# First loads of x and gate weights as one transfer each, with later loads held behind them, in a gated FFN on one core

## The reference

```
w = weights[conditions]                       # one 32x32 matrix per batch
y = einsum('bct,bcd->bdt', x, w)
h = silu(y @ w_gate) * (y @ w_up)             # 256 -> 1024
h_sparse = of each 4 neighbours, keep the 2 largest by magnitude
out = x + h_sparse @ w_down                   # 1024 -> 256
```

## Time and profile before

| | us |
|---|---|
| median of 3 runs | 83.6 (83.55 to 83.94) |
| the profiled execution's own time | 83.66 |
| its span (first to last instruction of the program) | 81.7 |
| PE busy | 75.5 (92%) |
| DVE busy | 61.2 (75%) |
| ACT busy | 42.9 (53%) |
| granted TensorE clock, mean | 0.994 of full |

### The profile page before, as it was taken

How to read it: one execution, slowest core, us unless ns; L and a number is a source line. 1 busy time by engine, 2 the same in 40 slices (tenths; PEclk the granted TensorE clock), 3 DMA queues, 4 the chain that set the end, 5 groups by cost and what they waited for, 6 DMA issues and landing times.

```text
span 81.7 us, 983 instructions
## 1 busy us (share of the span) xinstructions
PE 75.5 (92%) x338; PEld 59.8 (73%) x338; DVE 61.2 (75%) x93; ACT 42.9 (53%) x65; POOL 8.0 (10%) x13
## 2 busy tenths in 40 slices
PE   3996699999999999999999999999999999999920
PEld 1331688898888888888888888888888888888800
DVE  0003799178389999996899999999999999991060
ACT  6000983595863986975392699995770006410000
POOL 7500000000000070013000000442000000000000
PEclk9999999999999999999999999999999999999997
DMA  0792899977400049915800000399950000006024
GB/s 0 138 326 113 251 325 335 429 237 285 201 0 0 0 88 199 195 32 96 160 4 0 8 4 0 64 193 201 205 108 0 0 0 0 0 0 257 0 92 164
DMA packets 3076, 9.62 MB, mean 118 GB/s; under 512 B 480, under 2 KB 480, under 8 KB 2816
## 3 DMA queue, kind: packets, MB, share of 16 engines
q1 hardware_dynamic: 2160, 6.29, 22.3%
q0 software_dynamic: 912, 3.28, 20.9%
HBM read 5.37 MB, written 1.05 MB: 79 GB/s over the span
## 4 chain that ended last, share of the span: by engine, by line
PE 84%; DMA 8%; DVE 3%; ACT 1%; issue 1%; DVEq 0%
PE bank L536 50%; PE y_banks L573 13%; PE bank L573 13%; DMA h<-in_table,rows_sb 5%; PE y_banks L521 5%; PE bank L547 4%; DMA cond_sb<-in_cond 2%; DVE gate_raw L428 2%; ACT h L237 1%; DVE h L347 1%; DVE rows_sb L432 0%; DVEq L427 0%
## 5 line engine op out<-in xcount | busy, mean ns | idle before, releaser
L536 PE MATMUL bank<-y_hl,up_hl 128*128 128x512 f32 x96 | 24.2, 389 | 0.0
L536 PE MATMUL bank<-y_hl,gate_hl 128*128 128x512 f32 x84 | 21.4, 390 | 0.0
L536 PEld LDWEIGHTS bank<-y_hl,up_hl 128*128 128x128 f32 x96 | 18.0, 188 | 3.8
L536 PEld LDWEIGHTS bank<-y_hl,gate_hl 128*128 128x128 f32 x84 | 15.7, 188 | 3.2
L243 ACT ACTIVATE silu<-bank 128x512 f32<-128x512 f32 x16 | 9.4, 595 | 8.5 <-PE bank L536 8.2
L264 ACT ACTIVATE h_hl<-h 128x1024 fp32r<-128x1024 f32 (+1 forms) x8 | 6.7, 844 | 8.5 <-DVE h L414 8.4
L573 PE MATMUL y_banks<-h_hl,down_hl 128*128 128x512 f32 x48 | 11.0, 389 | 0.0
L573 PE MATMUL bank<-h_hl,down_hl 128*128 128x512 f32 x48 | 11.0, 389 | 0.0
L573 PEld LDWEIGHTS y_banks<-h_hl,down_hl 128*128 128x128 f32 x48 | 9.0, 188 | 1.9
L573 PEld LDWEIGHTS bank<-h_hl,down_hl 128*128 128x128 f32 x48 | 9.0, 188 | 1.9
L378 DVE TENSOR_TENSOR h<-bank,silu 128x512 f32<-128x512 f32 x12 | 8.1, 684 | 1.9 <-ACT silu L243 1.9
(11 more groups left out here) (40 smaller groups left out, 71.9 us busy)
## 6 DMA issues: line engine op xcount, KB each, us to landing
h_hl<-h POOLq DMA_DIRECT2D x4, 512.0 KB, 5.2
up_raw<-in_w_up SPq DMA_DIRECT2D x2, 512.0 KB, 5.8
down_raw<-in_w_down SPq DMA_DIRECT2D x1, 1024.0 KB, 9.5
gate_raw<-in_x_t SPq DMA_DIRECT2D x1, 1024.0 KB, 5.0
down_hl<-down_raw POOLq DMA_DIRECT2D x2, 512.0 KB, 5.5
out<-gate_raw SPq DMA_DIRECT2D x4, 256.0 KB, 2.3
x_sb<-in_x SPq DMA_DIRECT2D x2, 256.0 KB, 4.0
gate_raw<-in_w_gate SPq DMA_DIRECT2D x2, 256.0 KB, 4.4
```

What stands on the lines that cost most here:

```text
L536: last = nc.tensor.matmul(dst, w_hl[w][:, s, q, k, j], y_hl[:, m, half, k], start=i == 0, stop=i == len(terms) - 1)
```

## The change

The first half of x is loaded by one transfer of 128 x 4 KB pieces in place of two of 128 x 2 KB, and so are the gate weights of q = 0, with one semaphore for all of it. SP waits for those gate weights as well as for `mix_in` before it issues the up weights of q = 0, and then waits until these have landed before it issues the second half of x and what follows. ACT splits the gate weights ahead of its three blocks of the diagonal, and `WARM_START` goes from 18 to 16.

```diff
-    WARM_START = 18
+    WARM_START = 16
...
-        w_in = [[None, sem("gate_in1")], [sem(f"up_in{q}") for q in range(NQ)]]
-        first_in = [sem(f"first_in{k}") for k in range(KT)]
+        w_in = [[sem(f"gate_in{q}") for q in range(NQ)], [sem(f"up_in{q}") for q in range(NQ)]]
...
-            for g in range(0, GH, 2):
-                sp.dma_start(x_sb[:, g:g + 2, :], x[:, g:g + 2, :]).then_inc(x_in[0], 16)
-            for k in range(KT):
-                sp.dma_start(raw_w[0][:, 0, k], w_gate[:, 0, k]).then_inc(first_in[k], 16)
-
+            sp.dma_start(x_sb[:, 0:GH, :], x[:, 0:GH, :]).then_inc(x_in[0], 16)
+            sp.dma_start(raw_w[0][:, 0], w_gate[:, 0]).then_inc(w_in[0][0], 16)
+
+            sp.wait_ge(w_in[0][0], 16)
             sp.wait_ge(mix_in, 16)
             sp.dma_start(raw_w[1][:, 0], w_up[:, 0]).then_inc(w_in[1][0], 16)
+            sp.wait_ge(w_in[1][0], 16)
             sp.dma_start(x_sb[:, GH:NG, :], x[:, GH:NG, :]).then_inc(x_in[1], 16)
...
             def high_weights(q, w, k, end):
-                act.wait_ge(first_in[k] if (q, w) == (0, 0) else w_in[w][q], 16)
+                act.wait_ge(w_in[w][q], 16)
...
-            diagonal(ACT_FIRST)
             for piece in PIECES[:KT]:
                 high_weights(*piece)
+            diagonal(ACT_FIRST)
             for piece in Y_PIECES[:KT]:
                 high_y(*piece)
...
             def low_weights(i):
                 q, w, k, end = PIECES[i]
-                dve.wait_ge(first_in[k] if (q, w) == (0, 0) else w_in[w][q], 16)
+                dve.wait_ge(w_in[w][q], 16)
...
             def mixing(half):
-                pe.wait_ge(x_in[half], 32 if half == 0 else 16)
+                pe.wait_ge(x_in[half], 16)
```

## The result

The changed kernel takes 83.38 us (median of 14 runs, 83.02 to 83.72), the kernel before, run beside it, 83.86 (14 runs, 83.50 to 84.56). The ratio is 0.9948, with a 95% interval of 0.9925 to 0.9971: 0.44 us faster, between 0.24 and 0.63.

The account below looks back on a forecast made before the run. PE was taken to bound the kernel, its start held by the gather behind 1 MB of loads. Terms -0.55 +0 +0.2 +0 = -0.35 gave 83.3 from 83.66 and 83.25 from the median; forecast 83.2 us, range 82.6 to 84.0.

Parts of the forecast that it names:

- The reading that the gather stands in line: Start of the kernel: the gather is last behind 1 MB of x and gate weights and lands 0.35 us after them.
- The rival that the queues take turns: At the gather: it lands well ahead of the gate weights, PE starts at 8.1, time 82.9 us; chance 0.06.
- the rule that the prediction quotes for it: Trainium skill on DMA queues: each DMA engine takes turns between queues that have work, packet by packet.
- Part 1: First loads as one transfer each of 4 KB pieces: gather lands at 6.90, PE starts at 8.31, 0.55 us earlier.
- one slow stretch: First transfers from 2.2 to 4.3 us, moving 151 GB/s in the kernel before, against 295 in the later burst.
- the reading behind the 0.25: First loads: the slowness belongs to POOL's issue of the gather, so only the rest gets quicker, 0.25 us earlier.
- The reading behind the 0.85: First loads: they move like the later 1 MB burst in 4 KB pieces, landing at 6.25 for 7.1, 0.85 us earlier.
- Part 2: Gate splits ahead of the diagonal on ACT, before mixing(0): cost nothing, with 0.2 us of cover.
- Part 3: SP's wait for up weights before x's second half: up weights of q = 1 land at 17.5, PE waits 0.2 us at pair 3.
- The estimate from the Trainium skill: SP's later loads: 2.0 us plus bytes at 436 GB/s gives 3.2 us for up weights, 5.6 for the next 1.5 MB, no wait.
- Part 4: Two fewer matmuls on zeros at the start: PE idles 1.28 us before mixing(0); nothing gained, nothing lost.
- The rival of the clock: PE before mixing(0): without an earlier gather, 1.83 us idle could drop the clock to 1.2 GHz, 85.5 us; chance 0.02.

Follow-up runs that it names:

- The late gather: Kernel before with POOL zeroing the diagonal three times, so the gather is issued at 4.35 instead of 2.98; one execution, 83.77 us.
- diagonal first: Changed kernel with ACT's three blocks of the diagonal ahead of its gate splits, as before; 83.37 us, ratio 0.9942.
- the hold alone: Kernel before with only SP's added wait for the up weights ahead of the second half of x; 84.08 us, ratio 1.0032.
- four issues: Kernel before with x and gate weights of q = 0 in 4 KB pieces, two transfers of 64 partitions each; 84.92 us, ratio 1.0130.
- x alone: Changed kernel with only x's first half ahead of the gather, no held transfers, diagonal first, 14 matmuls on zeros; 84.66 us, ratio 1.0108.

## Why the prediction was right

**What bounds the start.** The reading that the gather stands in line behind what SP issued held with 0.75 MB and more ahead: 0.75 MB, 6.15; 1 MB, 6.85 to 6.95 in 4 KB pieces (7.30 in one execution) and 7.45 in 2 KB ones; 1.5 MB, 8.5; each about 0.35 behind the last of them. It does not reach further: with 0.5 MB ahead the gather lands at 6.17, 0.91 behind x, and issued 1.4 us later it takes 3.1 us. There the gather's own time is the limit, 3.1 to 3.2 us from its issue, which the prediction left out. It did no harm, as the gather issued at 2.98 was to land at 6.90. The rival that the queues take turns, and with it the rule that the prediction quotes for it, falls with 1.5 MB ahead: the gather had its 3.2 us behind it at 6.2, and still landed behind all of it.

**Part 1, 0.55 earlier.** Measured 0.50. The value was the middle of 0.25 and 0.85, two readings of one slow stretch. The late gather shows that the reading behind the 0.25 was false: the slowness does not belong to POOL's issue (that it has to do with POOL's other work isn't excluded, as POOL zeroed in that stretch). The reading behind the 0.85, the rate of the later burst (295 GB/s), was too high: the first burst reached 209. So the number came out right by luck, as a middle of two readings neither of which holds; the mechanism (4 KB pieces in one transfer move the first megabyte sooner, and the gather with it) did hold. What sets 209 against 295 is open. That the one-transfer loads do it is shown by the run with them alone. Whether it is the size of the pieces as such is not settled, as each other way of moving these bytes brought a cost of its own; fewer issues alone are not it.

**Part 2, ACT's order, nothing.** Right: diagonal first gives 83.37. The blocks came 0.18 behind DVE's copies, and the first was ready ahead of the third copy, as worked out. All three were done by 8.49, ahead of PE's third group near 8.86. (The prediction's 0.5 us to that group is two of eight groups' products, four rows of 16, not four of eight; the time is right.)

**Part 3, the hold, 0.2.** Measured 0.16 in the block of pairs, 0.26 and 0.30 in two other kernels with the hold, and 0.27 (0.02 to 0.51) in the time when the hold stands alone. The up weights took 3.5 us for 3.2 predicted, and those of q = 1 landed 6.75 behind the burst's first issue for 7.35: at 17.3 for 17.5 predicted. product(0) ended at 20.33 for 20.5. The estimate from the Trainium skill, DMA: Bandwidth & Descriptors, section Anatomy of one DMA (3.2 us and 5.6 us), was near for the first and 1.15 too short for the second, and would have left no wait where there was one.

**Part 4, two matmuls less.** No effect was seen; the runs with 18 and with 16 differ by less than they are uncertain. The clock stayed at its upper level across 1.37 us of idle time. The rival of the clock was a real one, though: the granted clock stayed at 1.00 across 1.90 us (the hold alone) and 2.16 us (the gather issued later), and fell behind 2.26 us (four issues) and 3.50 us (1.5 MB ahead). The 1.83 us that the rival had in mind lies under what was kept, but not far.

**The sum.** -0.35 predicted from -0.55 and +0.2; -0.36 in the traces from -0.50 and +0.16 (rest in small steps), -0.44 in the runs. The chances gave 0.45 to faster by over 0.5% and 0.43 to no change that can be told; the ratio lies on that edge.

## What to carry to other kernels

A small gather that the whole program waits for can land only when the bulk transfers issued ahead of it are done, and issuing it 1.4 us earlier didn't help. Its own time from issue to landing (3.2 us here) is the floor below which fewer bytes ahead gain nothing. So count the bytes ahead of it, move there only what the first instructions need, and give what must follow it a head start over the rest. A wait that holds back a queue costs nothing at its own place and must be priced at the far end: here four transfers, two splits, a silu and a product later. And a change made of several edits should be tried edit by edit: here one brought 0.5 us, one cost 0.1 to 0.3, and two did nothing that could be seen.

## What the runs showed of the hardware

- A gather of 128 KB issued by POOL behind transfers of SP landed about 0.35 us behind the last of these with 0.75, 1 and 1.5 MB ahead, and took 3.1 to 3.2 us from its issue where less was left ahead of it (x alone; issued at 4.35).
- Transfers of 64 partitions moved 235 GB/s from 4.3 to 6.5 us with the transfer engines busy all the time, against 337 (4 KB pieces) and 349 (2 KB) for 128 partitions (in an execution longer than most; the ratio too was 1.013).
- x alone (512 KB) landed at 5.26, and with 512 KB behind it at 5.3: the first transfer did not get quicker by being alone, whereas the k = 1 half of the gate weights took 3.7 us with 2 MB issued right behind it, and 3.15 with these held back for 1 us.
- The granted clock was 0.50 behind 2.26 us of idle PE and 0.70 (a mean over 3.1 us) behind 3.50 us; it stayed at 1.00 behind 1.37, 1.90 and 2.16 us.
